# GpSimd's elementwise work on a cross-attention and expert-layer kernel, written in column strips

## The reference

```python
q1 = fake_quant(layernorm(x), x1_scale, x1_zp)     # round, clip to 0..255
q2 = fake_quant(ctx, x2_scale, x2_zp)
x = x + tanh(g_xattn) * (q1 @ q2)                  # x is then "x1"

h = layernorm(x)
base = h @ base_W.T
w = weights of the top 2 of 8 experts (softmax of h @ router_W.T, renormalised)
inc = sum over experts of w[e] * (h @ lora_A[e]) @ lora_B[e]
x = x + tanh(g_ffn) * (base + 2 * inc)
```

## Time and profile before

| | |
|---|---|
| median of 3 executions | 1065.04 us (1063.71 to 1065.16) |
| the profiled execution | 1067.16 us, its span 1065.4 us |
| PE busy | 1020.5 us (96%), 5048 instructions |
| DVE busy | 793.7 us (74%), 1089 instructions |
| ACT busy | 482.1 us (45%), 503 instructions |
| POOL busy | 208.7 us (20%), 123 instructions |
| POOL L700, job steps | 32, 84.2 us |
| POOL L691, column terms | 64, 47.4 + 44.2 us |
| POOL L683, row terms | 16, 16.7 + 15.8 us |

### The profile page before, as it was taken

One profiled execution on the slowest core, in us unless ns is written; L12 is line 12 of the kernel. 1 busy time (PEld: TensorE's weight loads), 2 busy tenths in 40 slices (PEclk: granted clock), 3 DMA queues, 4 the chain that ended last, 5 costly groups with the idle time before them and its releaser, 6 DMA issues.

```text
span 1065.4 us, 13135 instructions
## 1 busy us (share of the span) xinstructions
PE 1020.5 (96%) x5048; PEld 770.3 (72%) x5072; DVE 793.7 (74%) x1089; ACT 482.1 (45%) x503; POOL 208.7 (20%) x123
## 2 busy tenths in 40 slices
PE   2999999999989999999999999999999999999998
PEld 1444444444878888888878878897787889888887
DVE  7999898996769562857687679967866897855554
ACT  7864785340432323234345435734444565433432
POOL 2345554669524160400000000000000000000000
PEclk9999999999999999999999999999999999999999
DMA  8794599556788869554767866867687586668765
GB/s 340 296 402 179 230 358 386 217 197 213 260 317 330 321 242 329 185 176 138 233 255 227 273 221 201 284 189 290 185 279 263 181 280 184 198 203 297 248 199 179
DMA packets 85198, 265.89 MB, mean 250 GB/s; under 512 B 7312, under 2 KB 15504, under 8 KB 77456
## 3 DMA queue, kind: packets, MB, share of 16 engines
q1 hardware_dynamic: 67472, 231.50, 62.2%
q10 hardware_dynamic: 17664, 33.56, 8.6%
HBM read 214.70 MB, written 50.33 MB: 249 GB/s over the span
## 4 chain that ended last, share of the span: by engine, by line
PE 73%; DVE 14%; DMA 7%; ACT 3%; issue 3%; SPq 0%; ACTq 0%; DVEq 0%
PE acc L1382 16%; PE acc L1397 15%; PE acc L1399 15%; PE acc L1398 15%; DVE w_lo L1090 4%; DMA w_stage<-in_wt 3%; DMA w_stage<-w_sums_scratch 2%; PE aT_psum L1467 2%; DMA out<-c_acc 2%; DVE S_sum L1223 1%; PE aT_psum L1446 1%; PE aT_psum L1445 1%; DVE S_lo L1231 1%; PE aT_psum L1369 1%; DVE c_acc L1201 1%
## 5 line engine op out<-in xcount | busy, mean ns | idle before, releaser
L1090 DVE TENSOR_TENSOR w_lo<-w_stage,w_hi 128x1024 fp32r<-128x1024 f32 x200 | 248.4, 1254 | 168.7 <-ACT w_hi L808 168.2
L808 ACT ACTIVATE w_hi<-w_stage 128x1024 fp32r<-128x1024 f32 x200 | 209.5, 1058 | 342.3 <-PE acc L1399 254.5
L1397 PE MATMUL acc<-w_hi,S_hi 128*128 128x512 f32 x384 | 151.4, 394 | 3.5 <-DVE w_lo L1090 3.1
L1399 PE MATMUL acc<-w_hi,S_lo 128*128 128x512 f32 x384 | 149.7, 390 | 0.0
L1398 PE MATMUL acc<-w_lo,S_hi 128*128 128x512 f32 x384 | 149.5, 389 | 0.0
L1397 PE MATMUL acc<-w_hi,A_hi 128*128 128x512 f32 x288 | 114.0, 396 | 0.3
L1382 PE MATMUL acc<-ctx_quant,aT_even 128*128 128x512 bf16 x501 | 112.5, 382 | 1.2 <-ACT aT_even L766 0.6
L1399 PE MATMUL acc<-w_hi,A_lo 128*128 128x512 f32 x288 | 112.4, 390 | 0.0
L1398 PE MATMUL acc<-w_lo,A_hi 128*128 128x512 f32 x288 | 112.2, 390 | 0.0
L1382 PE MATMUL acc<-ctx_quant,aT_odd 128*128 128x512 bf16 x499 | 111.0, 379 | 0.7
L700 POOL TENSOR_TENSOR t_job<-t_job 128x1024 f32<-128x1024 f32 x32 | 84.2, 2630 | 106.6 <-DMA t_job<-in_wt 105.3
(11 more groups left out here) (182 smaller groups left out, 1615.7 us busy)
## 6 DMA issues: line engine op xcount, KB each, us to landing
w_stage<-in_wt SPq DMA_DIRECT2D x104, 512.0 KB, 4.7
w_stage<-w_sums_scratch SPq DMA_DIRECT2D x96, 512.0 KB, 4.3
ctx_stage<-in_ctx SPq DMA_DIRECT2D x32, 1024.0 KB, 7.9
t_job<-in_wt SPq DMA_DIRECT2D x8, 2048.0 KB, 10.6
w_sums_scratch<-t_job SPq DMA_DIRECT2D x8, 2048.0 KB, 12.4
c_acc<-x_scratch SPq DMA_DIRECT2D x32, 512.0 KB, 6.2
out<-c_acc ACTq DMA_DIRECT2D x64, 256.0 KB, 5.5
x_rows<-x_scratch SPq DMA_DIRECT2D x11, 1024.0 KB, 8.1
```

Source lines behind the costliest of these rows:

```text
L808: ins = act.activation(wh[i % HI][:, :], raw[:, :], ACT.Copy)
L1090: ins = dve.tensor_tensor(low[:, :], raw[:, :], high[:, :].bitcast(F32), ALU.subtract)
L1397: pe.matmul(out_, lh, rh, start=first, stop=False, skip_group_check=onto)
L1399: return pe.matmul(out_, ll, rh, start=False, stop=final, skip_group_check=onto)
```

## The change

Each of the three kinds of GpSimd work is cut along its columns. A row term becomes four instructions of 512 columns, a column term two of 256, a job step four of 256. The numbers computed are the same. The waits stand before the first strip as they stood before the whole, and the semaphore is raised by the last strip. GpSimd's instructions in these three kinds go from 112 to 320. No other engine's instructions change, nor does any engine's order.

```diff
@@ -132,6 +132,7 @@
 HT = GT // 2
 SLOTS_G = 14
 JOBS = 8
+STRIP = 256
 GROUPS = (2, 0, 1, 3)
 JOBS_A = 3
 FILL_AT = (8, 9, 10, 11, 13, 14, 16, 17)
@@ -680,15 +681,20 @@
             def row_term(t):
                 pool.wait_ge(row_ready, t + 1)
                 tile = xg[(t // M) % 2][:, t % M, :]
-                pool.tensor_scalar(tile, tile, crow[:, t:t + 1], 1.0, ALU.add, ALU.mult).then_inc(xr_ready, 1)
+                for a in range(0, D, NW):
+                    part = tile[:, a:a + NW]
+                    ins = pool.tensor_scalar(part, part, crow[:, t:t + 1], 1.0, ALU.add, ALU.mult)
+                ins.then_inc(xr_ready, 1)
 
             def add_col_term(p):
                 t, c = UNITS[p]
                 n = c % NB
                 pool.wait_ge(colb_ready, c + 1)
                 pool.wait_ge(bank_read, p + 1)
-                blk = xg[(t // M) % 2][:, t % M, n * NW:(n + 1) * NW]
-                pool.tensor_tensor(blk, blk, colb[n][:, :], ALU.add).then_inc(x1_ready, 1)
+                for a in range(0, NW, STRIP):
+                    blk = xg[(t // M) % 2][:, t % M, n * NW + a:n * NW + a + STRIP]
+                    ins = pool.tensor_tensor(blk, blk, colb[n][:, a:a + STRIP], ALU.add)
+                ins.then_inc(x1_ready, 1)
 
             def t_step(j, i):
                 if i == 0:
@@ -697,7 +703,10 @@
                     pool.wait_ge(job_step, 4 * j + i)
                 b11, b21, b12, b22 = (job[j][:, a, :] for a in range(4))
                 to, left, right = ((b11, b12, b11), (b12, b22, b12), (b22, b22, b11), (b21, b21, b22))[i]
-                pool.tensor_tensor(to, left, right, ALU.subtract).then_inc(job_step, 1)
+                for a in range(0, WK * NW, STRIP):
+                    part = slice(a, a + STRIP)
+                    ins = pool.tensor_tensor(to[:, part], left[:, part], right[:, part], ALU.subtract)
+                ins.then_inc(job_step, 1)
 
             def t_job(j):
                 for i in range(4):
```

## The result

| | median | against the kernel before, 95% |
|---|---|---|
| before | 1063.53 us (22 executions, 1060.28 to 1067.18) | |
| with the change | 1066.58 us (22 executions, 1063.82 to 1068.03) | 1.0028 (1.0018 to 1.0039) |

The kernel became slower by 0.28%, some 3 us. I had forecast 3.5 us faster, a median of 1061.5 us with a range of 1058.6 to 1065.4. The profiled execution of the changed kernel took 1066.32 us, with a span of 1064.6 us; the one of the kernel before (1067.16) had been among its slowest.

The account below looks back on a forecast made before the run. TensorE, busy 96% of the span, was taken as the bound. Shorter waits before transposes (5.4 us) less GpSimd's lateness at the first stage's end (1.9) gave 3.5 us less: median 1061.5 us, range 1058.6 to 1065.4.

Parts of the forecast that it names:

- The tiny operations: VectorE's L1001, L1003 and L1004, on one number per partition: longest time under 1.0 us, where L1003 had 2.200.
- waits before the transposes: TensorE's waits until 108.45, 137.14 and 219.05 us shrink by 2.4, 0.8 and 2.2 us, together 5.4.
- wait on `ctx_quant`: TensorE coming earlier may wait for the context: cost zero, at most 1.5 us; new waits at 170 to 200 us would refute.
- the lateness of GpSimd: End of the first stage: ScalarE comes 2.1 and SyncE 1.9 us late; 1.9 us of loss, bounds 0 and 4.2.
- the strips: GpSimd's cost per cut: 0.15 us fixed per instruction; 0.69 us for 256 columns, row-term strips 0.49 plus 0.1 to 0.15.
- the step that failed: VectorE gets in at each boundary between GpSimd instructions, so a held operation waits at most one strip, 0.69 us.
- VectorE does not get in between strips: Rival, 8%: strips without a semaphore between them keep their hold, only the cost remains; 1.9 us slower, 1067.
- I am wrong if: Signs against: tiny operations over 1 us, new `ctx_quant` waits at 170 to 200 us, wait at 298.83 over 2 us longer.
- 298.83: Time in us of a wait whose growth by more than 2 us would show the forecast wrong.
- GpSimd is held in turn: Rival, 10%: VectorE takes turns at added boundaries, doubling GpSimd's 5.0 us of waits from 247.45 to 280.95; 1069 to 1070 us.

Follow-up runs that it names:

- e7: The changed kernel with one wait added, GpSimd for its own last column term before the first step of job 2: 1061.53 us, 0.9972 to before.
- e4: The changed kernel with GpSimd waiting for its own last column term before each job step and the reverse: 1059.89 us, 0.9962 to before.
- e1: The changed kernel with only row and column terms in strips, job steps whole: 1059.56 us, 0.9961 to before.
- e5: The changed kernel with jobs 1 to 7 whole; terms and job 0 stay cut: 1059.68 us, 0.9954 to before.
- e6: The changed kernel with only the row terms in strips: 1062.32 us, 0.9980 to before.
- e8: The changed kernel with one GpSimd wait for its own last column term, before the first step of job 1: 1066.79 us, 1.0023 to before.
- m2: Probe without the computation, varying strip count, width, semaphores, stops and PSUM input: at 256 columns the border lies between 14 and 15 strips.
- m1: Probe without the computation: GpSimd strips back to back, then three VectorE operations, 2.70 us with 12 strips of 256 ahead, 11.85 with 16.
- m3: Probe without the computation, testing VectorE turns and hold length behind back-to-back strips of 256: held 27.4 us with 40 strips behind.
- e2: The changed kernel with only the job steps in strips, row and column terms whole: 1069.28 us, 1.0028 to before.

## Why the prediction was wrong

**Right: what was won.** The tiny operations have a longest time of 0.72 us (forecast: under 1.0). All four waits before the transposes went. I had summed 5.4 us by 219 us; 6.0 were measured. No wait on `ctx_quant` came up in the changed kernel.

**Right in size: the lateness of GpSimd.** I took 2.1 us for ScalarE and 1.9 for SyncE; e7, where nothing covers them, shows 2.4 and 2.0. I made 1.9 us of loss for TensorE out of that; its waits for `hT_lo` at the step, 3.9 us before, are 5.0 in e7 and 5.6 in e4, so 1.1 and 1.7 us more. The forecast sum of 3.5 us less is about what the kernels without the hold give: 3.0 in e7, which is nearest to the changed kernel, 4.0 in e4 (0.38% of 1064), 4.2 in e1, 4.9 in e5.

**Off in size: the strips.** A strip of 256 was to take 0.69 us and takes 0.72 alone and 0.68 from one to the next. A row term's strip of 512 was to take 0.6 and takes 0.69 (its four 2.71 us where the whole took 1.97), so a row term grew by 0.74 us and not by 0.45.

**Missed, small: lateness in the middle of the stage.** I looked for it at the end only. At 221.31 us ScalarE's store waits for a column term that stands behind eight strips of job 0, the copy of `aT` behind that store is late, and TensorE idles 1.88 us. With its other small losses this takes back 2 of the 6 us: where it takes up the transposes of h, with one unit of the stage left, it is 4.0 us ahead (266.08 against 270.09). PE and then ScalarE in order of time:

```profile
223.75 2.54 PE L1391 MATMUL acc<-ctx_quant,aT_odd 128*128 128x512 bf16 x10 [1.88 <-issue]
...
221.78 1.88 ACT L775 ACTIVATE aT_odd<-aT_psum 128x2048 bf16<-128x2048 bf16 x1 [5.79 <-POOL x_group_even L696]
```

That the copy of `aT` is what TensorE waited for I read from these two rows, since the first names no engine. The other kernels bear it out: in e1 and e6, where job 0 is whole, the copy waits for TensorE's transpose and TensorE has no such wait; wherever job 0 is cut it has one, of 0.7 to 1.9 us.

**Wrong: the step that failed.** "VectorE is held for the rest of whatever GpSimd instruction is running, and gets in at the boundary between two of them even when the next is ready." The rows under it were five column terms in a row, and VectorE was let in at each boundary. Before the change GpSimd ran at most 7 instructions behind its last stop or VectorE's last turn when one of VectorE's waited for it. The change nearly triples the number of instructions (112 to 320) and adds no stop. It took the run ahead of L1094 to 19. In this region the rule of the rows doesn't hold: not one boundary lets VectorE in, and where I had costed a wait of up to 0.69 us stands one of 10.27 us. This one instruction costs TensorE 5.8 us without work and then nearly 7 us at half the clock.

The hold's price by the runs: e8 against e7 is 0.51%, 5.4 us; the change at 1.0028 against e4 at 0.9962 is 0.66%, 7.0 us, with intervals that leave 4 to 10. Forecast gain 3.5, less 5.4 to 7.0, is 1.9 to 3.5 us slower; 3 was measured.

**The rival that came near.** "VectorE does not get in between strips" was given 8% and 1067 us. The time fits, but not for its reason: it thought of strips without a semaphore between them, at every place, with the gain lost and only GpSimd's cost left. In fact the gain stayed, semaphores between strips change nothing (m2), and one hold at one place cost 5 to 7 us. I had asked what speaks against it and named the boundaries of the earlier trace rows; I had not asked how far the changed kernel would go beyond what those rows cover. "I am wrong if" was blind to it as well: it named the tiny operations, `ctx_quant` and 298.83, and not a large operation of VectorE at the join of the two stages.

**The other slow rival.** "GpSimd is held in turn" (10%, 1069 to 1070 us) did not come about. From 247.45 us to the end of job 2 GpSimd had 5.0 us of waits inside its instructions before; over the same work in e7 it has 4.1, not the double.

The Trainium skill (SBUF — State Buffer, "Who interferes with whom") says that the first to issue has the shared pair for the whole instruction and the other blocks fully. That covers the holds of before, but by it a held operation waits for one instruction; the 10.27 us go through fifteen. Of a VectorE instruction with at most one SBUF input, outside the modes that use both ports, it says that it doesn't contend; m2 agrees (0.44 us with the second input in PSUM, 11.15 with both in SBUF).

**What stays open.** Where the border lies. With 14 ahead VectorE was served in m1 and m2 and held in m3, whose run of 14 began behind three waits of GpSimd and not two; in e2 L1094 was held with 13 ahead, and job steps and column terms there have waits between them; the tiny operations of the changed kernel at 226 to 227 us were served with 13 to 15 ahead. Whether waits that are already met count along was not tested, nor what in the chip counts. In e1 a tiny operation (L1013) at 226.30 us took 2.01 us, through two boundaries to GpSimd's stop, at a count at which the changed kernel's was served; it may be the same thing at the border.

## What to carry to other kernels

Cutting GpSimd's instructions shortens what VectorE waits behind each, but raises the number that stand back to back: count them between two real stops, and keep that at 12 or fewer, where no trace here shows a hold past one boundary, or put in a wait of GpSimd for its own last result (0.15 us) ahead of the place where VectorE matters. A wait that is long met is no stop. When a price is read from rows, ask whether the changed kernel still lies in the region that those rows cover, here five instructions in a row and not nineteen.

## What the runs showed of the hardware

- After enough GpSimd instructions without a stop, a VectorE operation with both inputs in SBUF isn't let in at boundaries any more, as long as GpSimd goes on: 11.1 us with 16 strips behind, 27.4 us with 40. In the probes 13 ahead were served and 15 held, with 14 either way; in one kernel (e2) 13 were enough. With 12 or fewer it waited for one boundary.
- The number counts, not columns or time: 15 strips of 128 (6 us) hold, 14 of 512 (17 us) don't.
- A wait of GpSimd for its own result, 0.15 us, opens it again; semaphores that are met or raised do not.
- GpSimd's subtraction of 128x256 takes 0.72 us alone and 0.68 in a row, 128x512 1.26 and 1.22, 128x1024 2.34; an addition of one number per row to 128x512 takes 0.69 us.
